# Causal mask and row maximum in one VectorE instruction, FFN weights prepared by ScalarE, last half by quarters, new orders

## The reference

```python
q, k, v = x @ wq, x @ wk, x @ wv
q, k = fractional_rope(q), fractional_rope(k)      # rotates the first 64 of 128 columns by cos and sin
s = (q / sqrt(128)) @ (k / sqrt(128)).T - 1e30 * (i < j)
a = softmax(s) @ v @ wo
x = layernorm(x + a)
h = gelu(x @ bw1.T + b1)                           # bw = mean(|w|, axis=1) * sign(w), for w1 (512, 128) and w2 (128, 512)
x = layernorm(x + h @ bw2.T + b2)
```

## Time and profile before

| what | us |
|---|---|
| median of 3 runs (lowest, highest) | 291.37 (289.44, 291.97) |
| the profiled execution | 290.87 |
| its span, first to last instruction | 289.1 |
| mean granted TensorE clock | 0.971 |
| TensorE busy | 267.8 |
| VectorE busy | 231.7 |
| ScalarE busy | 228.7 |
| GpSimd busy | 166.3 |

### The profile page before, as it was taken

How to read it: one execution, slowest core, us unless ns; L and a number is a source line. 1 busy time by engine, 2 the same in 40 slices (tenths; PEclk the granted TensorE clock), 3 DMA queues, 4 the chain that set the end, 5 groups by cost and what they waited for, 6 DMA issues and landing times.

```text
span 289.1 us, 5187 instructions
## 1 busy us (share of the span) xinstructions
PE 267.8 (93%) x1531; PEld 211.5 (73%) x1531; DVE 231.7 (80%) x582; ACT 228.7 (79%) x390; POOL 166.3 (58%) x254
## 2 busy tenths in 40 slices
PE   8698799999999999999999999999999998999660
PEld 4577598897677868786888678867876777897430
DVE  2579979999987998789869896799799359254983
ACT  3366547637689778897899999689999989998992
POOL 3333215413343397376793988758829987899123
PEclk9969899999999999999999999999999999999995
DMA  7852462438639934573777237913693320202205
GB/s 183 144 75 59 127 78 48 87 78 189 177 76 238 171 56 94 133 175 75 119 172 177 69 77 200 224 24 82 174 224 88 84 72 1 73 2 73 73 3 145
DMA packets 58011, 31.94 MB, mean 110 GB/s; under 512 B 33408, under 2 KB 54400, under 8 KB 57984
## 3 DMA queue, kind: packets, MB, share of 16 engines
q1 hardware_dynamic: 57024, 30.76, 47.3%
q10 hardware_dynamic: 960, 0.85, 1.2%
HBM read 9.18 MB, written 4.19 MB: 46 GB/s over the span
## 4 chain that ended last, share of the span: by engine, by line
PE 83%; ACT 6%; DVE 5%; issue 4%; POOL 1%; ACTq 0%; POOLq 0%; DVEq 0%
PE pair L565 17%; PE bank L584 17%; PE bank L610 5%; PE bank L651 5%; PE bank L659 5%; PE bank L660 5%; PE bank L598 4%; PE pair L628 4%; PE pair L629 4%; ACT res L1051 3%; PE pair L668 2%; PE pair L641 2%; PE bank L617 2%; PE pair L643 2%; PE pair L642 2%
## 5 line engine op out<-in xcount | busy, mean ns | idle before, releaser
L378 POOL TENSOR_TENSOR hid_lo<-hid,hid_hi 128x1024 fp32r<-128x1024 f32 x28 | 66.4, 2389 | 27.8 <-ACT hid_hi L1024 27.8
L976 ACT ACTIVATE prob<-pair,negmax 128x128 f32<-128x128 f32 (+3 forms) x64 | 47.3, 742 | 18.8 <-DVE negmax L1430 15.1
L1430 DVE TENSOR_REDUCE negmax<-pair 128x1 f32<-128x128 f32 (+3 forms) x64 | 46.9, 748 | 12.0 <-PE pair L568 11.9
L584 PE MATMUL bank<-probT,xa 128*128 128x512 f32 (+3 forms) x160 | 54.7, 485 | 0.0
L584 PEld LDWEIGHTS bank<-probT,xa 128*128 128x128 f32 x160 | 28.9, 191 | 20.0 <-issue 15.6
L565 PE MATMUL pair<-qkT_hi 128*128 128x512 f32 (+3 forms) x96 | 39.5, 411 | 0.8 <-ACT tok L991 0.5
L1440 DVE STREAM_TRANSPOSE turned<-prob 128x128 f32<-128x128 f32 (+7 forms) x56 | 39.5, 725 | 0.6 <-ACT prob L976 0.6
L343 POOL TENSOR_TENSOR tok<-rot_cos,rot_sin 128x512 f32<-128x512 f32 x16 | 20.7, 1293 | 28.5 <-ACT tok L991 28.5
L565 PE MATMUL pair<-qkT_lo,qkT_hi 128*128 128x512 f32 (+3 forms) x96 | 33.3, 347 | 0.0
L565 PE MATMUL pair<-qkT_hi,qkT_lo 128*128 128x512 f32 (+3 forms) x96 | 33.3, 347 | 0.0
L1017 ACT ACTIVATE hid<-pair,b_sb,alpha 128x1024 f32<-128x1024 f32 x28 | 32.9, 1208 | 0.1
(11 more groups left out here) (117 smaller groups left out, 657.1 us busy)
## 6 DMA issues: line engine op xcount, KB each, us to landing
probT<-turned SPq DMA_DIRECT2D x96, 116.0 KB, 2.3
probT<-turned SPq DMA_DIRECT2D x128, 52.0 KB, 1.9
xq<-in_L_attn_x_dram SPq DMA_DIRECT2D x28, 128.0 KB, 3.7
xa<-in_L_attn_x_dram SPq DMA_DIRECT2D x7, 512.0 KB, 4.6
out_dram<-res SPq DMA_DIRECT2D x7, 512.0 KB, 3.2
hid<-in_L_ffn_w_dram SPq DMA_DIRECT2D x2, 256.0 KB, 3.2
out_dram<-res SPq DMA_DIRECT2D x2, 256.0 KB, 2.3
xa<-in_L_attn_x_dram SPq DMA_DIRECT2D x1, 256.0 KB, 3.6
```

The costliest lines, as they stand in the source:

```text
L378: pool.tensor_tensor(hid_lo[:, j, :], hid[:, j, :], hid_hi[:, j, :].bitcast(F32), ALU.subtract).then_inc(s_hid_lo[j], 1)
L584: ins = pe.matmul(bank_of["px", g, c][:, 0:n * P], xa[c % 2][:, j, :], probT[g][:, :, TG * j:TG * j + n, :].rearrange("p n m i -> p m n i" ...
L976: act.activation(prob[r % 3][:, 0:(r + 1) * P], pair_of["score", r, c][:, slice(*columns(r))], ACT.Exp, bias=negmax[:, r:r + 1], accum_out ...
L1430: dve.tensor_reduce(negmax[:, r:r + 1], pair_of["score", r, c][:, slice(*columns(r))], axis=AX.X, op=ALU.max, negate=True).then_inc(s_max[ ...
```

## The change

- The mask matmul is gone. `row_max` adds a row of zeros and -1e30 (`mask_row`, bf16, 1024 wide, the triangle in its last 128 columns) and reduces in the same instruction, which writes the sum times -1 back into the pair and takes the minimum; the exponential's scale becomes -1.
- `tok_copy` copies only the 64 columns that aren't rotated; `rotation_sum` waits for the products instead of the copy, and `turn_qk` for both. For element 0 VectorE does the two sums itself, and TensorE gets three more warming matmuls in front.
- Signs, magnitudes (Abs with the accumulator, scale 1/128 or 1/512) and the two copies of the turned signs move to ScalarE.
- The last element's second half goes in quarters of two tiles from the transposes of y to the second norm, with counters of their own (`s_lnq`), so that no means wait for GpSimd. The stores: tiles 4 and 5, then 0 to 3, then 6 and 7.
- The orders of all five queues are written anew.

```diff
...
+            tokens(1)
             stripes(2)
             carry(0, 0)
-            tokens(1)
             stripes(3)
...
-            store_half(0, B - 1)
-            store_half(1, B - 1)
+            store_part(1, B - 1)
+            store_part(0, B - 1)
+            store_part(2, B - 1)
...
             def rotation_sum(h, c):
-                pool.wait_ge(s_tok[h], c + 1)
+                pool.wait_ge(s_rot_mul[h], c + 1)
+                if c > 0:
+                    pool.wait_ge(s_qkT[2 * h + 1], c)
...
                     for n, (qp, kp) in enumerate(parts):
                         ins = pe.matmul(dst[:, lo:hi], qp[:, 0, me], kp[:, 1, lo - first:hi - first],
-                                        start=n == 0, stop=n == 2 and not diagonal)
-                    if diagonal:
-                        ins = pe.matmul(dst[:, hi - P:hi], ident_bf[:, :], mask_bf[:, :], start=False, stop=True)
+                                        start=n == 0, stop=n == 2)
...
             def turn_qk(n, c):
 
                 pe.wait_ge(s_rot_add[n // 2], c + 1)
+                pe.wait_ge(s_tok[n // 2], c + 1)
...
+            keep_warm(3)
             turn_qk(0, 0)
...
-                               bias=negmax[:, r:r + 1], accum_out=rowsum[:, r:r + 1]).then_inc(s_exp[r], 1)
+                               scale=-1.0, bias=negmax[:, r:r + 1], accum_out=rowsum[:, r:r + 1]).then_inc(s_exp[r], 1)
+
+            def setup_signs():
+                act.wait_ge(s_ffn_in, 16 * 4)
+                act.activation(sgn1, w1_sb, ACT.Sign).then_inc(s_signs, 1)
+                act.activation(sgn2, w2_sb, ACT.Sign).then_inc(s_signs, 1)
+
+            def setup_magnitudes():
+
+                act.wait_ge(s_ffn_in, 16 * 4)
+                for f in range(NF):
+                    act.activation(magnitude[:, 0, f * D:(f + 1) * D], w1_sb[:, f, :], ACT.Abs, scale=1.0 / D,
+                                   accum_out=alpha1[:, f:f + 1])
+                act.activation(magnitude[:, 1, :], w2_sb, ACT.Abs, scale=1.0 / H, accum_out=alpha2[:, 0:1]).then_inc(s_sums, 1)
...
-                act.activation(tok[:, TG * h:TG * (h + 1), :].rearrange("p n c -> p (n c)"), pair_of["qk", h, c][:, :],
+                act.activation(tok[:, TG * h:TG * (h + 1), :].rearrange("p n (j d) -> p n j d", d=D)[:, :, :, ROT:D],
+                               pair_of["qk", h, c][:, :].rearrange("p (n j d) -> p n j d", j=2, d=D)[:, :, :, ROT:D],
                                ACT.Copy).then_inc(s_tok[h], 1)
...
-                dve.tensor_reduce(negmax[:, r:r + 1], pair_of["score", r, c][:, slice(*columns(r))], axis=AX.X, op=ALU.max,
-                                  negate=True).then_inc(s_max[r], 1)
+                if r == 0 and c == 0:
+                    dve.wait_ge(s_const, 5)
+                mine = pair_of["score", r, c][:, slice(*columns(r))]
+
+                dve.tensor_tensor_reduce(mine, mine, mask_row[:, T - (r + 1) * P:T], -1.0, -MASKED, ALU.add, ALU.min,
+                                         negmax[:, r:r + 1]).then_inc(s_max[r], 1)
...
+            def second_means_quarter(q, c):
+                dve.wait_ge(s_stat2[1], c + 1 + q)
+                means(stat2, ln2, range(TG + 2 * q, TG + 2 * q + 2), s_lnq[q], 0)
...
+            def first_rotation_sum(h):
+                dve.wait_ge(s_rot_mul[h], 1)
+                four = tok[:, TG * h:TG * (h + 1), :].rearrange("p n (j d) -> p n j d", d=D)
+                dve.tensor_tensor(four[:, :, :, 0:ROT], rot_cos[:, h, :, :, :], rot_sin[:, h, :, :, :],
+                                  ALU.add).then_inc(s_rot_add[h], 1)
...
```

More of the change, by code:

```diff
@@ L165, in attention_ffn_kernel @@
         s_y_act, s_y_dve = sem("s_y_act"), sem("s_y_dve")
+        s_lnq = [sem(f"s_lnq{q}") for q in range(2)]
         s_xT_lo, s_rot_add, s_hid_lo, s_ln1, s_ln2 = (
@@ L644, in project, with turn_y_quarter @@
                 ins.then_inc(s_qk[h], 1)
+            def turn_y_quarter(q, c):
+                pe.wait_ge(s_yT[1], c + 1)
+                dst = next_bank("yTok", 1 + q, c)
+                for t in range(2):
+                    ins = pe.transpose(dst[:, t * P:(t + 1) * P], yT[:, (TG + 2 * q + t) * P:(TG + 2 * q + t + 1) * P],
+                                       ident[:, :])
+                ins.then_inc(s_yTok[1], 1)
             def turn_qk(n, c):
                 pe.wait_ge(s_rot_add[n // 2], c + 1)
+                pe.wait_ge(s_tok[n // 2], c + 1)
                 dst = next_bank("qkT", n, c)
@@ L1140, in _ @@
             exponentials(0, 3)
-            exponentials(1, 3)
+            tok_copy(1, B - 4)
+            xT_high(0, B - 3)
             pxT_copy(0, 2)
             x1T_high(0, 1)
+            exponentials(1, 3)
             exponentials(2, 3)
@@ L1204, in _ @@
+            exponentials(0, B - 3)
+            y_half(1, 1)
+            qkT_high(2, B - 3)
+            exponentials(1, B - 3)
+            hidden_high(0, 2)
+            second_norm(0, 0)
+            second_norm(1, 0)
+            qkT_high(3, B - 3)
+            second_norm(2, 0)
+            tok_copy(0, B - 2)
+            exponentials(2, B - 3)
+            exponentials(3, B - 3)
             second_norm(3, 0)
-            exponentials(0, B - 3)
-            exponentials(1, B - 3)
             pxT_copy(0, B - 4)
+            hidden_high(1, 2)
@@ L1232, in _ @@
             gelu(2, 3)
-            y_half(0, 2)
+            y_half(1, 2)
+            gelu(3, 3)
             qkT_high(2, B - 2)
-            gelu(3, 3)
-            y_half(1, 2)
+            second_norm(0, 1)
+            qkT_high(3, B - 2)
             exponentials(0, B - 2)
+            exponentials(1, B - 2)
+            exponentials(2, B - 2)
+            second_norm(1, 1)
             pxT_copy(0, B - 3)
-            exponentials(1, B - 2)
-            qkT_high(3, B - 2)
+            exponentials(3, B - 2)
@@ L1253, in _ @@
+            exponentials(5, B - 2)
             hidden_high(2, 3)
@@ L1496, in hidden_low_half, with means @@
                                   hid_hi[:, j, half(h)].bitcast(F32), ALU.subtract).then_inc(s_hid_lo[j], 1)
-            def means(stat, ln, h, done, before):
-                ts = slice(TG * h, TG * (h + 1))
-                for t in tiles(h):
+            def means(stat, ln, some, done, before):
+                ts = slice(some[0], some[-1] + 1)
+                for t in some:
                     ins = dve.bn_aggr(ln[:, 2:4, t], stat[:, t, :])
```

1029 lines of the change are left out of this document (509 added, 520 removed).

## The result

The changed kernel took 280.7 us in the median of 4 runs (277.6 to 282.1) against 291.7 us for the kernel before on the same chip: a ratio of 0.960, 95% interval 0.949 to 0.970. On a second chip the same kernel gave 279.4 against 292.4 (0.956, 0.952 to 0.961). The forecast was 282.3 us. The profiled execution took 280.73 us, its span 278.8, against 290.87 and 289.1.

What follows compares the result with a forecast made beforehand. TensorE was taken as the bound from 45 to 240 us. 290.87 - 5.3 (mask) + 1.0 (stalls) - 4.5 (start) - 0.3 (end) = 281.8, stated as 282.3 us for the median; range 277.2 to 288.5 us.

Steps and rivals of the forecast that it cites:

- The mask off TensorE: TensorE, 45 to 240 us: dropping mask matmuls saves 0.095 us per row, 5.3 us for 56 rows.
- Rival (d): Mask's slot on TensorE was hidden in weight loads; gain only 2.2 us, start 3; 286.9 us; chance 0.08.
- The mask on VectorE: Masked row maximum costs VectorE 0.1 us more each, 6.4 us in all; TensorE stalls 1 us, 0 to 4.
- (a): VectorE keeps the start, up to 80 us; maximum costs 0.2 us more, start gives 1.5; 287.3 us; chance 0.15.
- (c): Row maximum on VectorE at half rate, 0.6 us more per row, becomes the bound; about 298 us; chance 0.07.
- The start: 10 to 45 us: earlier rotation sums and FFN preparation off VectorE save 4.5 us, between 1.5 and 8.
- The copies of the rotation: ScalarE: shorter copies save 6.8 us, setups add 5.4; its total falls 1.4 us, relief late, load early.
- The orders: All five queues written anew: priced at 0, with 1 us to either side.
- The end: Last y half by quarters with counters of their own: 0.3 us gained, 0 to 1.
- Rival (b): Engines hand over without holes: 8 us at the start, no stalls, 0.7 at the end; 277.4 us; chance 0.15.
- the hole near 10 us: Sign of being right: TensorE's last projection-to-transpose hole, at the start, falls under 1.5 us.
- the clock: Sign of being right: TensorE's granted clock from 10 to 45 us rises above 0.95.

Runs made afterwards that it cites:

- e1: Changed kernel with only the mask put back on TensorE (mask matmuls and plain maximum): 286.0 us, ratio 0.977 to the kernel before.
- e3: Changed kernel with an extra reduction of 128 bf16 elements on VectorE before each row maximum: 284.5 us, ratio 0.974 to the kernel before.
- e10: Kernel before with only the sign and magnitude setups moved to ScalarE: 293.6 us against 292.0, ratio 1.009.
- e9: Changed kernel with the setups back on VectorE, placed later, and the signs' transposes moved later on TensorE: 286.2 us, ratio 0.981 to the kernel before.
- e6: Changed kernel with the first element's rotation sums back on GpSimd and without the three warming matmuls: 280.5 us, ratio 0.959 to the kernel before.
- e12: Changed kernel with ScalarE copying whole tokens again and the rotation's sums waiting for that copy: 286.1 us, ratio 0.979 to the kernel before.
- e4: Kernel with the new orders of all engines but every operation as in the kernel before: 296.0 us, ratio 1.014 to the kernel before.
- e11: Kernel before, in its old orders, with both the mask on VectorE and the setups on ScalarE: 290.3 us, ratio 0.996.
- e7: Changed kernel with the store of element 0 moved ahead of two token loads in SP's queue: 277.7 us, ratio 0.950 to the kernel before.
- e2: Kernel before, in its old orders, with only the mask moved to VectorE: 290.5 us against 293.1, ratio 0.996.
- e8: Changed kernel run again unaltered, on the chip of the experiments beside it: 279.4 us, ratio 0.956 to the kernel before.
- e5: Changed kernel with the sign and magnitude setups back on VectorE at their old places in its queue: 288.4 us, ratio 0.984 to the kernel before.

## Why the prediction came out

The forecast of 282.3 us lies 1.6 us above the median. The sum came closer than its steps: two of them failed, in opposite directions.

- **The mask off TensorE**, 5.3 us for 56 rows, 0.095 each: right. 0.089 each in the profiles, 6.0 us (3.6 to 8.4) in the times. Rival (d), the hidden slot, falls with e1. What the prediction lacked is the condition: in the old orders the same edit gave 1.2 us.
- **The mask on VectorE**, 0.1 us each and 1.0 us of stalls: mis-sized. The read takes no slot of its own (0.04 us at most), and no stall by the maxima came. (a) lost its ground with that; (c) too: 680 ns at 512 elements, not half rate. That VectorE had little cover was right: e3.
- **The start**, 4.5 us between 1.5 and 8: right in size. Up to element 2 the kernel with the mask still on TensorE is 4.8 us ahead of the kernel before (75.15 for 79.92). The bounds were loosely kept: the working ends at 8.5, the range at 8, and half way between 1.5 and 8 is 4.75. Its parts were less right: the estimate of 7 us of VectorE's work is confirmed (29.83 us busy against 22.69 without it, e10), and nearly all of it reached the end (e9). But the 1.5 us for the sum moved from GpSimd came out as 0.7, within the noise (e6), and the copy, for which only ScalarE's total was counted, is worth some 3 us there together with the sums' looser wait (e12). Undone one by one, mask, setups, sums and copy cost 20.4 us (e1, e9, e6, e12); undone together, with the quarters, 16.8 (e4 against the changed kernel). That they share holes, which single undos count twice, would explain it and isn't shown.
- **The copies of the rotation**, "the relief comes late": this step failed. Behind element 2, where nothing was counted for them, 3.0 us reach the end (e12). Whether that is the 6.8 us taken off ScalarE or the sums, which GpSimd may now begin before the copy, is not separated. The prediction's own row had the warning: ScalarE was busy for 143 of 160 us there, more than VectorE.
- **The orders**, "I price it 0, with 1 us to either side": this failed too, twice over. Alone they cost 4.0 us (e4), and without them mask and setups gave 1.2 together (e11). And SP's new order made a stall, 0.7 to 2.3 us, which e7 removes. The prediction looked at loads that pass copies, and not at the store that two loads pass. That the sum held is because the walk of the start used the new queues, and so priced orders and parts together, and because 2.3 us gained behind element 2 (e1 against before: 145.23 for 147.49) stand against the 2.3 us of the stall. That these two are alike in size is luck.
- **The end**, 0.3 us: 0 to 0.2 us by the two places shown above, at the low bound and too small for the times to tell. The last norms still waited for GpSimd; the quarters were not tried alone.
- **Rival (b)**, the hand-over works, had 277.4 us; e7 measured 277.7. Without stalls the number is reached, but not by its terms: e7 is 7.3 us ahead at element 2 with the mask's share in it, where 8 were to come from the start alone, the end gave 0.2 and not 0.7, and the rest came between elements 2 and 7 (5.8 us), from the copies too.

Of the signs named ahead: the hole near 10 us is 0.15 us (1.26 when the kernel was run again), the clock 1.00 (then 0.95, no longer above the 0.95 named), the transposes of rows 5 and 6 begin at 29.12 (row 7's at 31.3, just outside), a score matmul of 256 columns has its successor at 0.12 us when scores precede it, VectorE's total is 229.5, there are twelve table loads, none at Sign or the magnitudes. The signs against it stayed away: 0.68 us for the maximum at 512 elements, and no wait of TensorE for a maximum between 45 and 230 us.

Open: how much of the orders' part is due to each engine's order, whether e12's loss is the copy's length or the wait for it, and why the mask gave more in e11 than in e2.

## What to carry to other kernels

In a kernel whose queues are written by hand, the worth of an edit belongs to the edit and the order together: the mask was worth 6 us in one order and 1 to 4 in another (e1, e2, e11), and the order alone lost 4. So walk the new queues, not the old ones with one instruction changed; and ask of an engine at 90% on a stage what a shorter instruction frees there, or an engine that waits for it less, even when another engine is at 100%. For each store that moves in a queue, look up who writes its buffer next. Behind 1 MB of loads this store landed in 5.1 to 7.5 us (e1, e8, changed, e5), ahead of them in 5.1 (e7), and the stores in the median in 3.2; what the move gave for certain is an issue 3.8 us earlier (159.77 for 163.53).

## What the runs showed of the hardware

- A VectorE reduction with a second operand, writing PSUM back and leaving its result in an accumulator: 680 ns at 512 and 1219 ns at 1024 elements, as a plain reduction (677, 1210). Its read of 139 ns starts with the instruction that follows, and the slot grew by 0.04 us at most (0.47 us at 384 elements in both). ScalarE's read does take time of its own: 0.09 us, from 18.09 to 18.18 in the changed kernel's timeline, for a record of 0.21:

```profile
17.73 0.48 ACT L991 ACTIVATE prob<-pair,negmax 128x256 f32<-128x256 f32 x1
18.09 0.21 ACT L991 ACTIVATION_READ_ACCUMULATOR prob<-pair,negmax 128x1 f32 x1
18.18 0.64 ACT L1020 ACTIVATE xT_hi<-xT 128x512 fp32r<-128x512 f32 x1
```

- Freed slots of TensorE came back as idle time in the old order (e2): 2.6 us of 160 where it had none.
- The clock granted from 10 to 45 us was 0.85 for the kernel before and 1.00 and 0.95 for the changed kernel in its two profiles, in which TensorE had waited 0.15 and 1.26 us for the first sum. It was 1.00 for e7 after 0.67 us, 0.95 for e1 after 0.53, and 0.90 for e6 and e12 after 1.9 and 1.4. The end of e6 was later by 0.7 us (1.8 to either side), and its span was the 278.8 of the changed kernel: what a clock of 0.90 in that stage costs is below what these times show.
